# Fetching a sheared term 64 rows per transfer instead of 32, in an attention layer between two feed-forward layers

## The reference

```python
dist = clip(arange(s)[:, None] - arange(s)[None, :], -128, 128) + 128
rel_pos = rel_emb[dist]                                  # (s, s, 8), a table of 257 rows
scores = einsum('bhqd,bhkd->bhqk', q, k)                 # 16 heads of 8 dims, s = 512
scores = scores + einsum('bhqd,qkd->bhqk', q, rel_pos)   # the relative term
attn = softmax(scores / sqrt(8))
local_ctx = einsum('bhqk,bhkd->bhqd', attn, v)
out = gate * local_ctx + (1 - gate) * global_attn        # then @ Wo.T + bo
```

## Time and profile before

| | us |
|---|---|
| median of three runs | 3011.84 |
| profiled execution, its own time | 3018.18 |
| its span (first to last instruction) | 3016.4 |
| PE busy in the span | 2784.3 (92%) |
| DVE, ACT, POOL busy | 1893.3, 1737.2, 1393.2 |
| 324.94 MB moved by DMA, mean | 108 GB/s |

### The profile page before, as it was taken

The page is one execution under the profiler, slowest core; times in us unless marked ns, Lnnn a source line. Parts: engine busy times, 40 slices in busy tenths (PEclk is TensorE's granted clock), DMA queues, the critical chain, the costliest instruction groups (busy, mean ns, idle before and its releaser), DMA issues. The chain is left out here.

```text
span 3016.4 us, 60252 instructions
## 1 busy us (share of the span) xinstructions
PE 2784.3 (92%) x18624; PEld 2007.5 (67%) x18624; DVE 1893.3 (63%) x4781; ACT 1737.2 (58%) x3222; POOL 1393.2 (46%) x1728
## 2 busy tenths in 40 slices
PE   5999999999489999999998988999997999999999
PEld 4777777777155665555565555665565777777777
DVE  7666666667246666555665555665556666666666
ACT  4565565665255565555565555655555565565665
POOL 2554554554434434444434444444423555554554
PEclk9999999999589999999999999999997999999999
DMA  4000000000477777777777776777751000000000
GB/s 112 1 0 0 0 0 0 0 0 1 120 202 219 211 212 219 216 202 216 213 215 209 213 199 198 217 223 219 203 162 49 8 3 7 7 3 7 7 3 11
DMA packets 233801, 324.94 MB, mean 108 GB/s; under 512 B 29444, under 2 KB 188548, under 8 KB 233604
## 3 DMA queue, kind: packets, MB, share of 16 engines
q1 hardware_dynamic: 194436, 171.36, 22.9%
q0 software_dynamic: 36864, 150.49, 14.9%
q10 hardware_dynamic: 2304, 0.61, 0.1%
HBM read 141.68 MB, written 154.92 MB: 98 GB/s over the span
## 5 line engine op out<-in xcount | busy, mean ns | idle before, releaser
L1076 DVE CUSTOM_DVE_ANT_0 at_junk<-at_ps_s,at_rel 128x512 bf16<-128x512 f32 x1024 | 666.5, 688 | 477.4 <-PE at_ps_s L756 320.1
L893 ACT ACTIVATE at_probs<-at_ps_t 128x512 f32<-128x512 f32 x1024 | 559.4, 595 | 589.4 <-PE at_ps_t L741 588.9
L378 POOL TENSOR_TENSOR ffn_h_lo<-ffn_h,ffn_h_hi 128x512 fp32r<-128x512 f32 x384 | 502.0, 1311 | 477.7 <-ACT ffn_h_hi L305 477.7
L489 DVE TENSOR_TENSOR ffn_h<-ffn_silu,ffn_ps_gate 128x512 f32<-128x512 f32 x576 | 393.6, 683 | 409.7 <-ACT ffn_silu L348 407.6
L305 ACT CAST ffn_h_hi<-ffn_h 128x512 fp32r<-128x512 f32 x576 | 359.0, 623 | 406.7 <-DVE ffn_h L489 405.2
L741 PE MATMUL at_ps_t<-tab_ident,at_rel 128*128 128x128 f32 x3328 | 503.5, 292 | 0.0
L194 PE MATMUL ffn_ps_mid<-ffn_xT_hi,ffn_w_mid 128*128 128x512 f32 x1152 | 481.5, 418 | 21.3 <-DVE ffn_h L489 11.5
L194 PE MATMUL ffn_ps_gate<-ffn_xT_hi,ffn_w_gate 128*128 128x512 f32 x1152 | 457.8, 397 | 0.0
L194 PE MATMUL ffn_ps_out<-ffn_h_hi,ffn_w_out 128*128 128x512 f32 x1152 | 454.4, 395 | 0.2
L741 PEld LDWEIGHTS at_ps_t<-tab_ident,at_rel 128*128 128x128 f32 x3328 | 377.7, 147 | 87.6 <-issue 31.8
L348 ACT ACTIVATE ffn_silu<-ffn_ps_mid 128x512 f32<-128x512 f32 x576 | 344.3, 598 | 82.9 <-PE ffn_ps_gate L194 76.4
(11 more groups left out here) (161 smaller groups left out, 3980.9 us busy)
## 6 DMA issues: line engine op xcount, KB each, us to landing
at_band<-at_src POOLq DMA_DIRECT2D x256, 574.0 KB, 4.8
at_rel<-at_band SPq DMA_DIRECT2D x512, 143.5 KB, 3.8
at_qs<-at_q_hi SPq DMA_DIRECT2D x128, 64.0 KB
at_ks<-at_k_hi SPq DMA_DIRECT2D x128, 64.0 KB
at_rel<-at_band SPq DMA_DIRECT2D x64, 128.0 KB, 3.2
at_rel<-at_band SPq DMA_DIRECT2D x64, 127.5 KB, 3.2
at_rel<-at_band SPq DMA_DIRECT2D x64, 112.0 KB, 2.9
at_rel<-at_band SPq DMA_DIRECT2D x64, 111.5 KB, 4.3
```

Of the source, the lines that this page charges most:

```text
L378: pool.tensor_tensor(h_lo[:, u % RH, :], h[:, u % RH, :], h_hi[:, u % RH, :].bitcast(F32), ALU.subtract).then_inc(hlo_pool.sem, 1)
L489: dve.tensor_tensor(h[:, u % RH, :], silu[:, u % RH, :], ps_gate[:, u % 2, :], ALU.mult).then_inc(h_done.sem, 1)
L893: act.activation(probs[:, kp, 2 * hp + i].rearrange("p n q -> p (n q)"), ps_t[:, i, :], ACT.Exp).then_inc(exp_done.sem, 1)
L1076: dve.tensor_tensor_reduce(out=junk[:, i, :], in0=ps_s[:, i, :], in1=rel[:, c % RREL, l, h, :], scale=1.0, scalar=-3e38, op0=ALU.add, op1= ...
```

## The change

One transfer of `fetch_rel` covers GROUP = 64 rows instead of 32, two transfers make a block instead of four, and the margin PAD grows from 31 to 63 numbers. So the row that POOL writes grows from 287 to 319 numbers a head, and the row of `band` from 318 to 382. The semaphore of a block counts to 32 instead of 64. `fill_far` has 32 columns fewer to fill, since the fetched row is 32 wider. Everything else stays.

```diff
-    PAD = 31
+    GROUP = 64
+    PAD = GROUP - 1
     WIDE = BAND + PAD
     HEADW = PAD + WIDE
     PITCH = HG * HEADW
@@
-        rel_in = [ring(f"rel_in{i}", 64) for i in range(4)]
+        rel_in = [ring(f"rel_in{i}", 32) for i in range(4)]
@@ send_band, and in the same way maximum (DVE)
-                    pool.wait_ge(r_ring.sem, r_ring.at(n, 64))
+                    pool.wait_ge(r_ring.sem, r_ring.at(n, 32))
@@ fetch_rel
-                for g in range(4):
-                    first = P - 1 - 32 * g if qb == 0 else 0
-                    last = BAND - 1 - 32 * g if qb == QPB - 1 else WIDE
-                    key = P * (qb - 1) + 32 * g + 1 + first
-                    row = ((2 * c + l) % 4 * P + 32 * g) * PITCH
-                    rows = bass.AP(band, row + PAD + first, [[PITCH - 1, 32], [HEADW, HG], [1, last - first]])
-                    sp.dma_start(rel[32 * g:32 * g + 32, c % RREL, l, :, key:key + last - first], rows).then_inc(r_ring.sem, 16)
+                for g in range(P // GROUP):
+                    first = P - 1 - GROUP * g if qb == 0 else 0
+                    last = BAND - 1 - GROUP * g if qb == QPB - 1 else WIDE
+                    key = P * (qb - 1) + GROUP * g + 1 + first
+                    row = ((2 * c + l) % 4 * P + GROUP * g) * PITCH
+                    rows = bass.AP(band, row + PAD + first, [[PITCH - 1, GROUP], [HEADW, HG], [1, last - first]])
+                    sp.dma_start(rel[GROUP * g:GROUP * g + GROUP, c % RREL, l, :, key:key + last - first], rows).then_inc(r_ring.sem, 16)
```

More of the change, by code:

```diff
@@ L1068, in maximum @@
                     r_ring, n = rel_ring(c, l)
-                    dve.wait_ge(r_ring.sem, r_ring.at(n, 64))
+                    dve.wait_ge(r_ring.sem, r_ring.at(n, 32))
                 if k == 0:
```

## The result

The changed kernel is slower: a median of 3037.62 us (five runs, 3032.83 to 3044.09) against 3011.84 for the kernel before, a ratio of 1.0086, 95% interval 1.0064 to 1.0108. Measured a second time, it was 3054.89 against 3011.93, 1.0126 (1.0105 to 1.0147). The forecast was 2988, the range ended at 3019. The profiled execution is the fastest of the five, 3032.83 us with a span of 3031.0, so the two traces differ by 14.65 us and explain that much, not all of the 26.

The account below looks back on a forecast made before the run. It took the attention as bound by PE's own work, its idle waits at A and B, and half-clock losses. A +3, B -12.5, clock -12 and maxima -2 made -23.5 us: 2988 from 3011.84, range 2968 to 3019.

Parts of the forecast that it names:

- SP's issue: SP's DMA queue: two issues a block instead of four, 1.25 us a block, 0.9 us saved.
- Place B: Item 6, second block, each sequence: DVE's wait for the fetch shrinks 2.4 us; 12.5 of PE's 13.7 us go.
- 12 of clock: Dips to PE's half clock after B: of about 14 us lost, 12 us won back.
- The fetch in a quiet place: Fetches away from A and B: start 0.3 to 0.6 us later, issued 0.9 sooner, about even or sooner.
- Place A: Item 5, second block, each sequence, fetch behind the q spread: wait +0.2 us, +3 us over 15 sequences.
- The maxima: PE's waits for maxima behind a fetch in SP's order, 8.2 us in 4 waits: 2 us won.
- POOL and ACT: Band's write behind POOL's copy: write takes 0.2 to 0.5 us more; ACT's longer wait for `src` stays hidden.
- Bytes: Band write 11.1% more, all reads together 9.7%; DMA share 0.74 to about 0.80, row packets growing in proportion.
- The slower one: Rival: DMA engines become the bound after A, DVE waits at ordinary items; +25 us, 3037; chance 0.16.
- No change: Rival: issues take twice 433 ns or SP is held; 3017, or 3009 with half of B's gain; chance 0.20.
- the rival of the smaller A: Rival: A is issue-bound and shrinks too, -11 us instead of +3, about 5 of clock; 2969; chance 0.14.

Follow-up runs that it names:

- lone fetches: Fetches only, no layer computed, four blocks in each of eight forms: at 319 numbers, 14.10 us with 32 neighbouring rows, 14.61 with 64.
- every second partition: Changed kernel with its two 64-row transfers sent to every second partition, rows misplaced: 2999.20 us, 0.9931 of the kernel before.
- write and read wide: Kernel before with PAD = 63 alone, 319 numbers written and read, still four transfers of 32 rows: 3040.05 us, 1.0088.
- every fourth: Kernel before with its four 32-row transfers each sent to every fourth partition, rows misplaced: 3097.10 us, 1.0268.
- write wide: Kernel before with rows written 319 numbers wide, fetch still four transfers of 32 rows and 287 numbers: 3023.35 us, 1.0039.
- 0, 2, 1, 3: Kernel before with a block's four 32-row transfers issued in this order, neighbours in the queue going to different partition halves: 3020.92 us, 1.0000.
- lots: Kernel before with the q and k spread DMAs dealt in lots over slots 2 to 5, partly ahead of the second fetch: 2983.00 us, 0.9900.
- split: Kernel before with the 24 q and k spread DMAs dealt over slots 2 to 5, all behind the second fetch: 3124.63 us, 1.0378.

## Why the prediction was wrong, point by point

- **SP's issue.** Forecast 1.25 us a block, 0.45 an issue. An issue takes 0.617 us. A's block took 1.35 us in the mean (2.20 before), so the saving there was almost as forecast. But the block behind it, the first of item 6, took 2.06 us for 2.21: there SP was held for nearly all that it should have saved. A's issue to B's shrank by 0.90 us, not by 1.8. The loads of x at 472 ns were the wrong stand-in. 128 rows take 448 ns in the lone fetches as well, and 64 take longer: the time does not follow the count of pieces.
- **Place B is the step that failed.** Forecast: B's wait shrinks by 2.4 us, 12.5 us of waiting and 12 of clock are won. Measured: 2.25 became 2.50 us of DVE's wait, PE's waits at B went from 13.7 to 17.1 us, and of the clock's 12 us some 3 came (an estimate: in the whole attention PE is busy at the half clock for 151.6 us instead of 157.7, and half of that is lost). The issue came 0.90 us sooner, and issue to landing grew by 1.12 (6.65 to 7.77), where the forecast had 0.7 less for its own two transfers and 0.3 more for bytes. The runs put the growth on the bytes (with 32 rows and 319 numbers 7.49) and on the half (every second partition: 5.98). Step by step, PE's waits at B are 13.7 us before, 29.8 with the bytes of "write and read wide", 17.1 in the changed kernel and 3.7 with every second partition. So the saved issues did win at B, and the bytes had cost more than they won.
- **The fetch in a quiet place.** Forecast about even or sooner. Issue to landing went from 5.51 to 6.06 us although the issue itself was 0.76 shorter. Nothing followed at DVE there, as forecast: 31 waits before and after.
- **Place A** was right: 7.22 became 7.48 us, forecast +0.2. PE's waits there went from 84.0 to 88.1 us, forecast +3.
- **The maxima** gave 7.7 us instead of 2. SP comes to them sooner; with slower issues (*every fourth*) the same wait is 24.9 us.
- **POOL and ACT.** Forecast: the band lands 0.2 to 0.5 us later and ACT hides it. It lands 0.55 later (4.93 to 5.48 in the mean), and ACT's cover was not enough: 12 us of PE in one trace, 22 in the other. The prediction had named this price and put it at nothing. With the same wide write and 32 rows it would have been nearly right (0.5 us of PE in "write wide"); the wait came with the 64 rows.
- **Bytes.** "The row packets grow in proportion" and the share of 0.80 are what the bytes did with 32 rows (56 ns for 51, share 0.80). What the sum had no term for is where the 64 rows go: 86 ns and 0.84. And it priced the bytes at 0.3 us of B's landing, where they cost 0.84 (6.65 to 7.49) with 32 rows.
- **The rivals.** The slower one gave 3037 and came true at 3037.62, with 0.16 of chance. That it came so near is luck, as the repeat's 3054.89 shows; its mechanism was half right. Later landings of the band and the fetch ate B's gain; but the new PE wait came through ACT and `src`, not through DVE at ordinary items, and the first trace has no new dips of the clock. "No change" was right that SP is held at A. The Trainium skill's advice to prefer 32 partitions to 64 ("SBUF — State Buffer", The DMA setup-cost knee: "same bandwidth, half the SBUF") stood in the prediction as a remark beside the rival of the smaller A. The lone fetches agree with it as far as it goes (179 and 185 GB/s). A rival should have been made of it, with a price for rows that go to one half of the partitions. Two of the prediction's sums do not come out, either. Half of B's gain beside +5 us is -7, not -3; and its own bounds (B nothing, A +9, the maxima -2) reach 3019, not the 3004 that it gives as its own range.

**The sum.** Forecast +3 - 12.5 - 12 - 2 = -23.5 us. The traces have +7.5 (PE for DVE: A +4.1, B +3.4), +11.8 (PE for ACT) and -7.7 (maxima), which is +11.6 us of idle time, with an estimated -3 for the clock beside it, against 14.65 measured. So some 16 us of the miss are at B's waits, 12 at ACT and 9 at the clock. The size also depends on the execution. The repeat's trace has 9 us more of PE waiting for ACT than the first, and 195 us at the half clock, where the first had 164 and the kernel before 174. That goes with its larger loss (43 us in the medians, for 26), but what makes one execution dip more than another was not found.

**What is shown.** Three things by runs that change one thing each. The bytes alone, with 32 rows, cost as much as the whole change did in its first measurement (1.0088 and 1.0086). Merging to 64 neighbouring rows at those bytes wins nothing on balance (1.0086 and 1.0126), though it saves issues. And with 64 rows, the placement alone is worth 47 to 59 us.

**Open.** Why 64 partitions, or a step of four, take 0.6 us to issue, and 32 or all 128 neighbours 0.43 to 0.45. Also, how much the half costs 32 rows in the kernel. Their packets of 1148 bytes take 84 ns alone in the order 0, 1, 2, 3 and 51 in 0, 2, 1, 3, but in the kernel 51 in both. The 64 neighbours stay at 86 in the kernel (102 alone), where every second partition has 55. So in the median the packets to 32 neighbours are as quick in the kernel as in the alternating order, and those to 64 are not; in the mean 32 neighbours are at 82.9 ns for 1276 bytes, 64 at 90.3 and every second at 69.0. That one transfer keeps its half busy twice as long while the band's write asks for all partitions is argued, not shown. A fetch of all 128 rows in one transfer was not tried in the kernel.

## What to carry to other kernels

When transfers are merged, ask where the merged one's rows go as well as how many issues go away: look at issue to landing of the whole block, not at the count of issues. Merging that needs padding is paid twice, in the write and in the read, and larger transfers can also hold up whoever waits for the write's buffer; sum the padding's bytes against the share of the DMA engines before counting saved issues. Where one engine issues everything, a reordering moves the wait to something else. It won 1% where what was moved came a little late (*lots*), and lost 3 to 4% where it came 6 to 7 us late (*split*).

## What the runs showed of the hardware that was not expected

- SP's issue of a fetch with four pieces a row: 432 ns for 32 neighbouring rows, 605 for 32 at every fourth partition, 617 for 64 (neighbours or every second), 448 for 128.
- SP's issue of the next block can be held: the block behind A's took 2.06 us with two transfers, where a block elsewhere takes 1.38.
- Alone, 64 rows of 319 numbers over all partitions move at 246 GB/s, into one half after the other at 179; 32 neighbouring rows of 287 numbers at 189, and at 217 when the halves alternate. In the kernel that alternation changed nothing (1.0000), and the step of two was worth 1.5 to 2% of the whole time.
